# Round loops of four engines, written out as straight programs with constant waits

## What is computed

```python
def reference(x, adj, ...):                      # x [32, 512, 128], adj [512, 512]
    x = _layernorm(x + _L0_gnn_ref(x, adj, ...))  # attention: exp(8 tanh(x q k^T x^T / (8 sqrt(128)))) * adj, rows summed to 1, times x v
    x = _layernorm(x + _L1_gnn_ref(x, adj, ...))  # edge gates: sigmoid(tgt_i + src_j) * mask, aggregation, two dense layers with elu
    x = _layernorm(x + _L2_gnn_ref(x, adj, ...))  # Chebyshev: relu(x W0 + L x W1 + T2(L) x W2 + bias)
    x = _layernorm(x + _L3_gnn_ref(x, adj, ...))  # five gated steps: m = adj h; z, r, hv from m and h; h = (1-z) h + z hv
    return x
```

## Time and profile before

| | |
|---|---|
| median of 3 runs | 2019.74 us (2018.72 to 2021.35) |
| the profiled execution | 2019.12 us |
| its span in the trace | 2016.9 us |
| mean granted clock of TensorE over the span | 0.975 |
| share of the span in which TensorE's matmuls are busy | 92% |
| busy time of DVE, ScalarE, GpSimd | 73%, 67%, 46% |

### The profile page before, as it was taken

How to read it: one execution, slowest core, us unless ns; L and a number is a source line. 1 busy time by engine, 2 the same in 40 slices (tenths; PEclk the granted TensorE clock), 3 DMA queues, 4 the chain that set the end, 5 groups by cost and what they waited for, 6 DMA issues and landing times.

```text
span 2016.9 us, 27720 instructions
## 1 busy us (share of the span) xinstructions
PE 1857.0 (92%) x9419; PEld 1446.4 (72%) x9419; DVE 1470.6 (73%) x3054; ACT 1354.4 (67%) x2689; POOL 924.1 (46%) x1009
## 2 busy tenths in 40 slices
PE   3999998899998999889998899989999899999997
PEld 2767776777767778577785777858778577776775
DVE  6786678666887677866678667786677766778766
ACT  1756677476775767657685667856678567686666
POOL 2354444344453453634436344463444534445444
PEclk6999999999999999999999999999999999999999
DMA  2000001000010000100000000100001000000000
GB/s 70 21 1 1 1 1 43 2 1 1 1 42 2 1 1 6 37 2 1 1 17 27 2 1 1 43 1 2 1 1 43 1 1 1 1 22 1 1 1 22
DMA packets 13525, 21.46 MB, mean 11 GB/s; under 512 B 2720, under 2 KB 5024, under 8 KB 13216
## 3 DMA queue, kind: packets, MB, share of 16 engines
q1 hardware_dynamic: 10768, 18.68, 2.7%
q10 hardware_dynamic: 2576, 0.53, 0.1%
HBM read 10.82 MB, written 8.39 MB: 10 GB/s over the span
## 4 chain that ended last, share of the span: by engine, by line
PE 67%; DVE 12%; issue 8%; POOL 7%; ACT 6%; DMA 0%; POOLq 0%; DVEq 0%; ACTq 0%; SPq 0%
PE psA L1068 7%; PE psA L1069 7%; PE psA L1098 7%; PE psB L895 5%; PE psB L896 5%; PE psB L897 5%; PE psA L890 5%; PE psA L895 4%; PE psA L897 3%; PE psA L896 3%; PE psB L966 3%; PE psA L966 3%; DVE E L762 2%; PE psA L993 2%; PE psB L1091 2%
## 5 line engine op out<-in xcount | busy, mean ns | idle before, releaser
L439 POOL TENSOR_TENSOR S<-S,H 128x512 f32<-128x512 f32 x160 | 225.5, 1409 | 448.9 <-ACT S L582 448.9
L1068 PE MATMUL psA<-adjT_hi,nh_hi 128*128 128x512 f32 x640 | 266.6, 417 | 9.4 <-ACT H L568 9.4
L480 ACT ACTIVATE X<-X,shift,rstd 128x128 f32<-128x128 f32 x512 | 210.4, 501 | 90.2 <-POOL shift L410 89.0
L1069 PE MATMUL psA<-adjT_hi,nh_lo 128*128 128x512 f32 x640 | 253.1, 395 | 0.0
L434 POOL TENSOR_TENSOR xT_lo<-H,xT_hi 128x512 fp32r<-128x512 f32 x160 | 219.2, 1382 | 69.6 <-ACT xT_hi L590 37.6
L850 DVE SCALAR_TENSOR_TENSOR E<-E 128x512 f32<-128x512 f32 x160 | 180.8, 1130 | 59.3 <-ACT E L586 56.2
L845 DVE SCALAR_TENSOR_TENSOR E<-E,H 128x512 f32<-128x512 f32 x160 | 126.3, 790 | 115.1 <-ACT E L576 114.7
L405 POOL TENSOR_TENSOR neg_mean<-zero_cols,mv 128x4 f32<-128x4 f32 x128 | 28.4, 222 | 346.3 <-DVE mv L705 345.0
L688 DVE TENSOR_TENSOR gT_lo<-psA,gT_hi 128x512 fp32r<-128x512 f32 x160 | 108.8, 688 | 94.1 <-ACT gT_hi L572 94.1
L1098 PE MATMUL psA<-E,u5T 128*128 128x512 f32 x320 | 164.4, 595 | 3.2 <-DVE E L845 3.2
L580 ACT ACTIVATE E<-psB,z_bias 128x512 f32<-128x512 f32 x160 | 110.2, 689 | 78.3 <-PE psB L1092 77.2
(11 more groups left out here) (226 smaller groups left out, 5349.1 us busy)
## 6 DMA issues: line engine op xcount, KB each, us to landing
xin<-in_x SPq DMA_DIRECT2D x32, 256.0 KB, 3.0
out<-X SPq DMA_DIRECT2D x32, 256.0 KB, 2.0
E<-in_adj SPq DMA_DIRECT2D x1, 1024.0 KB, 5.9
E<-in_L_gnn_w_w SPq DMA_DIRECT2D x3, 128.0 KB, 6.8
E<-in_L_gnn_weight SPq DMA_DIRECT2D x1, 192.0 KB, 6.4
E<-in_L_gnn_u_w SPq DMA_DIRECT2D x2, 64.0 KB, 6.6
Wm_sb<-in_L_gnn_Wm ACTq DMA_DIRECT2D x1, 128.0 KB, 6.2
E<-in_L_gnn_q SPq DMA_DIRECT2D x1, 64.0 KB, 5.6
```

The source lines that it names most:

```text
L439: nc.gpsimd.tensor_tensor(kept[s], kept[s], H[s][:, :], ALU.mult).then_inc(pool_done[s], 1)
L480: last = nc.scalar.activation(X[s][:, t, :], X[s][:, t, :], ACT.Identity, scale=rstd[s][:, t:t + 1], bias=shift[s][:, t:t + 1])
L1068: nc.tensor.matmul(psA[s][:, :], hi, adjT_hi[:, m, :], start=(m == 0), stop=False)
L1069: last = nc.tensor.matmul(psA[s][:, :], lo, adjT_hi[:, m, :], start=False, stop=(exact and m == TILES - 1))
```

## The change

On each of the four engines the loop of the chip becomes a loop of the language that writes the program, so the seven passes over the cyclic order are written out one behind the other. `r` is now a number in all of them; the waits hold constants, and the instructions that worked out values in registers and closed the loop are gone. The order of the work on each engine is the same. TensorE's program for an inexact adjacency is written out in the same way.

```diff
             run("gpsimd", stages, 0, first=True)
-            with pool.Fori(1, ROUNDS) as r:
+            for r in range(1, ROUNDS):
                 run("gpsimd", stages, r)
             run("gpsimd", stages, ROUNDS, last=True)
...
             run("scalar", stages, 0, first=True)
-            with act.Fori(1, ROUNDS) as r:
+            for r in range(1, ROUNDS):
                 run("scalar", stages, r)
...
             run("vector", stages, 0, first=True)
-            with dve.Fori(1, ROUNDS) as r:
+            for r in range(1, ROUNDS):
                 run("vector", stages, r)
...
                 run("tensor", stages, 0, first=True)
-                with pe.Fori(1, ROUNDS) as r:
+                for r in range(1, ROUNDS):
                     run("tensor", stages, r)
                 run("tensor", stages, ROUNDS, last=True)
```

## The result

The changed kernel takes 1994.3 us (median, 1990.77 to 1996.3), the kernel before 2020.16 us on the same chip: a ratio of 0.9872, 95% interval 0.9858 to 0.9886, or 25.9 us less. The forecast was 1995 us. The profiled execution took 1990.77 us, its span is 1988.7 us.

The account below looks back on a forecast made before the run. TensorE, its matmuls busy 92% of a 2016.9 us span, was taken as the bound. Seven rounds of 241.89 us save 24.6 us, other loops and registers nothing: 2019.74 - 24.6 = 1995.1, rounded 1995 us, range 1989 to 2002.

Parts of the forecast that it names:

- The taken jumps: TensorE's six jumps back to `cheb01`: 17.44 us with a jump, 13.33 without, so 4.11 us each.
- The second hole: TensorE's further idle time of 1.62 us, three matmuls after the first hole (2.92 us) behind a jump.
- The clock's share: The remaining 1.29 us of a jump's cost: granted clock 0.50 from 867.5 to 874 us after TensorE stood idle.
- the exit: The last pass, branch not taken: 1.72 us idle at the same place, ended by DVE's xT_lo, and no second hole.
- The whole round: Period without a jump, mean of 241.50 and 242.28 us, taken for all seven: 24.6 us less than 1717.8.
- the fall in `edges`: Clock at 0.93 on the mean from 332 to 358 us in the longer of two jump-free periods, 242.28 us.
- The other three loops: Jumps of DVE, ScalarE and GpSimd, ahead of L845, L480 and L434: covered or without idle time, counted as nothing.
- The registers: Instructions working out wait values in the loops: taken as 0, 12 us less kept as the far end.
- No change: Rival: a branch costs only its instruction, 83 ns, and idle time returns as waiting for xT_lo; 2019.2 us; 3%.
- the seams: Rival: each of 79 instruction pieces in the straight program costs TensorE 1.62 us; some 2123 us, slower; 3%.
- The clock's rival: Rival: clock falls in `edges` or at `cheb01` take part back, 1.29 us in each of six rounds; 2005.6 us; 7%.
- The registers as the larger effect: Rival: register instructions were on the path after all, 12 us below the forecast; 1983 us; 3%.

Follow-up runs that it names:

- e2: The changed kernel with TensorE's loop kept, the other three engines written out: 2018.85 us, ratio 0.9991 to the kernel before.
- e8: The changed kernel with ScalarE's loop kept and its jump moved from ahead of L480 to the start of `cheb23`: 2015.13 us, ratio 0.997.
- e9: The changed kernel measured once more, all four engines straight, beside the same kernel before (2020.58 us): 1994.11 us, ratio 0.9868.
- e10: The kernel before with only TensorE's loop written out, run again beside the changed kernel: 1996.99 us, ratio 0.9887.
- e11: The kernel before with all loops kept and TensorE's jump announced by a hint, run again beside the changed kernel: 1997.32 us, ratio 0.9887.
- e1: The kernel before with only TensorE's loop written out, first run: 1998.53 us against 2021.19, ratio 0.9885.
- e3: The kernel before with loops kept and a hint near the top of TensorE's loop body announcing its jump, first run: 1998.82 us, ratio 0.9895.

## Why the prediction was right, step by step

**The taken jumps, 4.11 us each: right.** At the same place the changed kernel takes 13.34 us where it took 17.44. That was one jump of six, and one with short holes; over all six, the stretch from L775 to L828 lost 26.5 us, 4.4 us a jump. The second hole was taken away by itself by the loop's place in the code, both holes together by the hint. The clock's share went with them; no run took it away alone. The wait for xT_lo came back as the exit had shown.

**The whole round, 241.89 us: right in mechanism, a little off in size.** The period measured 241.40 us, 0.49 us below the mean that I took and 0.10 below my lower end. I gave half of the rounds the fall in `edges`; in the changed kernel's trace that fall stands in round 0 alone, at 93 us, ahead of the first L426, so none of the seven periods has it. Two of the signs that I named came out otherwise. The clock at `cheb01` was not 1.00 in every round (0.74 in rounds 4 and 5). And two periods, 240.93 and 240.98 us, lie below the 241 us that I had put to the registers; but these are rounds with the faster of the lap's two paces (last section), worth 0.5 us, and the 241.50 us that I took for the shortest period was one with the slower. The sum by one execution was 24.6 us; the medians say 25.9, the profiled spans 28.2. That the median came within 0.7 us of 1995 is partly luck: the sum gave 1992.3 us for the span, and the two traces of the changed kernel have 1988.7 and 1992.4 us.

**The other three loops, nothing: right, and for the reason given.** e2 bounds them, with the registers and beside TensorE's jumps, to 3.6 us, and the waits that covered them stand in the changed kernel too, the first unchanged, the second 0.15 us shorter than in the earlier trace rows:

```profile
949.61 2.80 DVE L845 SCALAR_TENSOR_TENSOR E<-E,H 128x512 f32<-128x512 f32 x4 [2.92 <-ACT E L576]
```

```profile
882.60 1.65 ACT L480 ACTIVATE X<-X,shift,rstd 128x128 f32<-128x128 f32 x4 [7.27 <-POOL shift L410]
```

e8 shows that the cover mattered: a jump of ScalarE without one cost over 2 us a round.

**The registers, nothing: a flawed comparison.** I laid the last round from L426 to L854 beside the one before it, as constants beside registers. But only TensorE had left its loop by then. DVE's first instruction behind its exit is L845 at 1944.01 us, so most of that stretch still ran with DVE's registers. Equal times could not show what they cost. It is about 0.2 us a round, on DVE or GpSimd. The forecast's far end of 12 us covered it; the step itself rested on rows that couldn't carry it.

**The rivals.** No change is out: 25.9 us. For the seams: 76 packets came in, near the 79 that I had estimated, and none of TensorE's matmul groups has idle time by issue in the changed kernel's trace; a straight program pays nothing to be seen. The clock's rival came true in part: the clock fell at `cheb01` in two rounds of this trace, and in three of e9's, the same kernel. But a fall cost 0.5 us there and not the 1.29 us that I had reckoned with, so it took back about 1 us. The registers as the larger effect are out as well: with them gone and the jump kept (e2) the time stays within 0.2%.

## What to carry to other kernels

On the engine that bounds the kernel, a jump back over a whole round, or forward over 600 matmuls, cost about 4 us a pass: the hole itself, a second one where the target's piece of code ends, and the lower clock that follows. Look for it as idle time by issue in the group that stands first in a loop's body, and compare the first pass and the exit with the passes between. On TensorE writing the loop out and announcing the jump did the same (e10 and e11); on the other engines it was enough that the loop turns where the engine waits anyway.

## What the runs showed of the hardware beside

**The lap's matmuls have two paces at the full clock.** In the stage behind `cheb23` the matmuls of L1039 and L1040 (128 a round) take 14.47 us in some rounds and 15.03 us in others, 113.9 or 118.3 ns from one to the next, in both kernels. Two windows of the changed kernel, in rounds 3 and 4 (length, busy and matmuls, clock):

```profile
868.00:880.00 12.00, 12.00 (x109) 1.00 0.01 2
1109.50:1121.50 12.00, 12.00 (x104) 1.00 0.00 1
```

TensorE is never idle in either and the granted clock is 1.00 in both, yet one holds 109 matmuls and the other 104. It makes 0.5 us a round, by no rule that I found: the kernel before had the fast pace in two of its eight rounds, the changed one in four and, as e9, in five, e1 in one and e10 in none. What sets it stays open.

**A store of the round before can reach DVE.** L734 writes X, which a store of the round before to `out` may still read. In a round of e1 it waited 2.48 us for that store, in the changed kernel 0.48 us at the same place, but in e9, the changed kernel once more, 2.10 us; e3 waits about 1 us in five of its rounds, once 1.31 us.

```profile
802.94 0.61 DVE L734 SCALAR_TENSOR_TENSOR X<-psA,rsum,xin 128x128 f32<-128x128 f32 x2 [2.48 <-DMA out<-X]
```

```profile
798.05 0.61 DVE L734 SCALAR_TENSOR_TENSOR X<-psA,rsum,xin 128x128 f32<-128x128 f32 x2 [0.48 <-DMA out<-X]
```

```profile
810.79 0.61 DVE L734 SCALAR_TENSOR_TENSOR X<-psA,rsum,xin 128x128 f32<-128x128 f32 x2 [1.31 <-DMA out<-X]
```

So one such wait doesn't tell two kernels apart. In e3 and e11, where the waits of about 1 us come in most rounds, the stretch that holds them is 4 to 5 us longer in the sum than in the changed kernel. Why the store comes later there no run shows.
